# A decoder layer on one core: score products on 64 rows of the array, and a tile's turned queries copied in one operation

## What is computed

```python
q = (x @ Wq + bq).reshape(1, B * N, H, hd)          # H = 16 heads of hd = 16
kv = (cond @ Wkv + bkv).reshape(1, -1, 2, H, hd)
...
q = _fq_sym(q, axis=-1)      # per query and head: integers of -127..127 times a scale
k = _fq_sym(k, axis=-1)
v = _fq_sym(v, axis=2)
attn = jnp.einsum('bhqd,bhkd->bhqk', q, k)          # 2048 queries x 2048 keys, per head
attn = jax.nn.softmax(attn.astype(jnp.float32), axis=-1)
attn = _fq_unsigned(attn, axis=-1)
out = jnp.einsum('bhqk,bhkd->bhqd', attn, v)
```

## Time and profile before

| | |
|---|---|
| runs shown | 1208.26, 1210.47, 1211.15 us |
| median | 1210.47 us |
| the profiled execution's own time | 1209.02 us |
| its span on the core | 1207.2 us |
| VectorE, TensorE, ScalarE, GpSimd busy | 82%, 79%, 73%, 69% |
| TensorE's granted clock, mean | 0.955 of full speed |

### The profile page before, as it was taken

The page is one execution under the profiler, slowest core; times in us unless marked ns, Lnnn a source line. Parts: engine busy times, 40 slices in busy tenths (PEclk is TensorE's granted clock), DMA queues, the critical chain, the costliest instruction groups (busy, mean ns, idle before and its releaser), DMA issues.

```text
span 1207.2 us, 30185 instructions
## 1 busy us (share of the span) xinstructions
PE 958.1 (79%) x11255; PEld 700.0 (58%) x11424; DVE 989.7 (82%) x1865; ACT 884.3 (73%) x1085; POOL 838.9 (69%) x890
## 2 busy tenths in 40 slices
PE   7966678787887878787887878787887878778886
PEld 4644446565665656566665656565665656656565
DVE  4878778797988878797988878797988878798983
ACT  2636677778787778778787778777787777778782
POOL 7678777777777887777877887777777877733030
PEclk9967899899999999999999999899999989999997
DMA  5001000000000000000000000000000000000000
GB/s 200 2 35 40 6 1 6 2 10 2 6 7 5 7 1 11 2 6 6 6 6 7 6 2 10 1 6 6 6 7 6 7 1 6 2 6 2 6 2 10
DMA packets 8439, 14.00 MB, mean 12 GB/s; under 512 B 1635, under 2 KB 6246, under 8 KB 7910
## 3 DMA queue, kind: packets, MB, share of 16 engines
q1 hardware_dynamic: 8294, 12.06, 3.0%
HBM read 9.96 MB, written 2.10 MB: 10 GB/s over the span
## 4 chain that ended last, share of the span: by engine, by line
PE 40%; ACT 20%; issue 19%; DVE 17%; POOL 2%; DMA 0%; DVEq 0%; ACTq 0%; SPq 0%; POOLq 0%
PE ps_score L1479 10%; DVE score L1103 10%; PE ps_score L1468 9%; ACT prob L797 9%; ACT prob_t L809 8%; PE ps L1332 7%; PE ps_pv L1495 5%; DVE prob_t L1120 2%; PE ps_score L1332 2%; DVE early L1170 2%; ACT routed_both L848 1%; PE ps L1421 1%; ACT queries L782 1%; DVE stats L1026 1%; PE ps L1518 1%
## 5 line engine op out<-in xcount | busy, mean ns | idle before, releaser
L1103 DVE TENSOR_SCALAR_CACHE_REDUCE score<-ps_score,q_neg 128x1024 f32<-128x1024 f32 x512 | 642.9, 1278 | 147.9 <-PE ps_score L1468 145.4
L797 ACT ACTIVATE prob<-score,exp_bias 128x2048 uint16<-128x2048 f32 x256 | 513.9, 2007 | 14.9 <-DVE exp_bias L1113 14.9
L1468 PE MATMUL ps_score<-keys,queries 128*128 128x512 bf16 x855 | 281.5, 396 | 193.4 <-ACT prob_t L809 121.5
L1479 PE MATMUL ps_score<-ident_f,prob 128*128 128x128 f16 x4096 | 280.7, 223 | 16.7 <-ACT prob L797 8.8
L1479 PEld LDWEIGHTS ps_score<-ident_f,prob 128*128 128x128 f16 x4096 | 250.9, 100 | 50.2 <-ACT prob L797 22.5
L809 ACT COPY prob_t<-ps_score 128x1024 int32<-128x1024 int32 x192 | 194.3, 1012 | 55.2 <-PE ps_score L1479 53.3
L1468 PEld LDWEIGHTS ps_score<-keys,queries 128*128 128x128 bf16 x1024 | 68.3, 99 | 258.2 <-issue 162.7
L543 POOL TENSOR_TENSOR folded<-product 128x512 f32<-128x512 f32 x128 | 160.0, 1273 | 6.3 <-DVE ho L1062 4.3
L533 POOL TENSOR_TENSOR product<-hs_exp,v_tok 128x1024 f32<-128x1024 f32 x64 | 148.8, 2348 | 12.3 <-ACT hs_exp L765 12.3
L533 POOL TENSOR_TENSOR product<-qk_rot 128x1024 f32<-128x1024 f32 x64 | 148.9, 2347 | 4.0 <-POOL qk_rot L526 4.0
L1495 PEld LDWEIGHTS ps_pv<-prob_t,values 128*32 128x32 f16 x4096 | 114.8, 97 | 54.5 <-issue 54.4
(11 more groups left out here) (145 smaller groups left out, 1256.6 us busy)
## 6 DMA issues: line engine op xcount, KB each, us to landing
prob_t<-in_w SPq DMA_DIRECT2D x3, 1024.0 KB, 4.8
x_in<-in_x SPq DMA_DIRECT2D x16, 128.0 KB, 2.0
score<-in_cond_t SPq DMA_DIRECT2D x4, 512.0 KB, 6.8
out<-x_out SPq DMA_DIRECT2D x16, 128.0 KB, 1.7
w_qkv<-in_w_qkv SPq DMA_DIRECT2D x1, 768.0 KB, 4.0
early<-in_w_kv SPq DMA_DIRECT2D x1, 512.0 KB
w_s<-in_w_s SPq DMA_DIRECT2D x3, 128.0 KB
w_o<-in_w_o SPq DMA_DIRECT2D x1, 256.0 KB
```

The lines of the kernel that those rows point to most:

```text
L797: act.activation(prob[:, s, :].bitcast(U16), score[:, s, :], ACT.Exp, bias=exp_bias[:, s:s + 1], scale=-1.0, accum_out=prob_sum[:, t.par, ...
L1103: dve.tensor_scalar(score[:, s, HALF * i:HALF * i + HALF], ps_score[:, slot(h, i)].rearrange("p b k -> p (b k)"), q_neg[:, t.par, h:h + 1] ...
L1468: mm = pe.matmul(ps_score[:, slot(h, i), b, :], queries[:, t.par, h // 2, h % 2, :], keys[:, h // 2, k0:k0 + KEYS], start=True, stop=True)
L1479: mm = pe.transpose(out[:, P * i:P * i + P], prob[:, h % RING, P * i:P * i + P], ident_f16[:])
```

## The change

The score products read 48 partitions of keys and queries, 0 to 47 for an even head and 64 to 111 for an odd one; in the built program each of them uses 64 rows of the array by 128 columns, rows 0 to 63 or 64 to 127. `queries` loses its axis j and its zeros, the memset with its semaphore goes, and `keep_queries` is one copy of 128 partitions. `q_kept` counts one per tile where it counted two.

```diff
-        queries = sb("queries", [P, 2, H // 2, 2, P], BF16)
+        queries = sb("queries", [P, 2, H // 2, P], BF16)
...
-            pool.memset(queries[:].rearrange("p r a j q -> p (r a j q)").bitcast(F32), 0.0).then_inc(rows_cleared, 1)
...
-                if t.starts():
-                    act.wait_ge(rows_cleared, 1)
-                for j in range(2):
-                    rows = slice(P // 2 * j, P // 2 * j + P // 2)
-                    act.copy(queries[rows, t.par, :, j, :], bank_bf[5][rows, :].rearrange("p (a q) -> p a q", q=P)
-                             ).then_inc(q_kept, 1)
+                act.copy(queries[:, t.par].rearrange("p a q -> p (a q)"), bank_bf[5]).then_inc(q_kept, 1)
...
-                    pe.wait_ge(q_kept, t.count(2, 2))
+                    pe.wait_ge(q_kept, t.count(1, 1))
...
+                rows = slice(P // 2 * (h % 2), P // 2 * (h % 2) + 3 * HD)
                 for b in range(2):
                     k0 = HALF * i + KEYS * b
-                    mm = pe.matmul(ps_score[:, slot(h, i), b, :], queries[:, t.par, h // 2, h % 2, :],
-                                   keys[:, h // 2, k0:k0 + KEYS], start=True, stop=True)
+                    mm = pe.matmul(ps_score[:, slot(h, i), b, :], queries[rows, t.par, h // 2, :],
+                                   keys[rows, h // 2, k0:k0 + KEYS], start=True, stop=True)
```

More of the change, by code:

```diff
@@ L309, in layer_kernel @@
         q_kept = sem("q_kept")
-        rows_cleared = sem("rows_cleared")
         sum_inverted = sem("sum_inverted")
@@ L1553, in experts @@
                     if (t + 2).exists():
-                        pe.wait_ge(q_kept, (t + 2).count(2, 2))
+                        pe.wait_ge(q_kept, (t + 2).count(1, 1))
                 if i == 1 and j == 1:
```

## The result

The changed kernel takes 1262.0 us (median of four runs, 1257.7 to 1275.5) against 1210.6 us before: 1.045 times as long, with a 95% interval of 1.041 to 1.049. The forecast was slower, 1228 us, with a range up to 1252; the loss is 51.4 us where 17.5 were predicted.

What follows compares the result with a forecast made beforehand. No engine alone bounds the kernel; the chain of waits does, TensorE on 40% of it. 1209.0 - 15.8 + 29.1 + 4.5 = 1226.8, plus 1.5 to the median: 1228 us; own range 1214 to 1245, with rivals 1204 to 1252.

Steps and rivals of the forecast that it cites:

- the copy: ScalarE at h = 13: one of two turned-queries copies goes, 1.0 us a tile, wholly on the path, -15.8 us.
- Its cover on TensorE's side: q_turn and gate product, next to become late, are delayed 0.2 us; copies start from an exponential's end, without idle time.
- The memset's 1.8 us: GpSimd at 5.2 us of the span loses this work, but the loads hide it: 0.
- The price of a place: TensorE, each change of array shape: +0.11 us with 16-bit weights behind it, +0.19 us with float32 weights.
- How many places are on the path: Shape changes on the chain: 63 entries after 128 x 128 products, 125 exits (105 float32, 20 16-bit), +29.1 us.
- a tenth of the work off the chain: Of the other 46 us of shape changes, where the chain runs over VectorE and ScalarE, one tenth counts: +4.5 us.
- the clock: Rival: half-row products make TensorE's granted clock fall more often, about 1.1 us a tile, 18 us: 1246 us; chance 0.10.
- No price for 64 rows: Rival: 64-row score products on TensorE need no priced change of shape, so the kernel takes 1195 us; chance 0.11.
- the draw: Rival: float32 exits cost 0.11 and waits cover half the places; 10 us added, about 1210 us; chance 0.12.
- Weights in the open within a pair: Rival: second score product's weight load isn't hidden, 0.05 to 0.1 us per pair, +7 to +15, about 1239 us; chance 0.07.

Runs made afterwards that it cites:

- VectorE's half and the filling: Kernel before, with VectorE copying the upper 64 partitions of turned queries and 8 unread products added at h = 15 of each tile: 1182.8 us, 0.978.
- the split copy: Kernel before, with VectorE copying the upper 64 partitions of the turned queries at the end of h = 14, ScalarE the lower: 1200.2 us, 0.992.

## Why the prediction was right and wrong

**What bounds the kernel; the copy.** Right. One copy of 1.00 us instead of two, the whole block behind it moves forward, and the stall keeps its 3.33 us. The term was -15.8 us (16 x 1.0 is 16.0; the 0.2 matters nowhere). Undoing it costs some 14 in the changed kernel, and tiles at full clock go from 67.34 to 66.20 with the one copy and to 66.18 with VectorE's half and the filling, 1.16 a tile or 18.6 us for 16. Its cover on TensorE's side (q_turn and the gate product) held, with no idle time ahead of the copy at 645.65. The memset's 1.8 us went into a wait: GpSimd stands 8.3 us ahead of `rope`'s first step where it stood 6.6.

**The price of a place.** Right, to 0.01 us: 0.11 with 16-bit weights, predicted 0.19 and found 0.20 with float32. It was carried over from 32 rows and 32 columns, and 64 rows and 64 columns pay the same. The weight load of a score product no longer comes ahead of it, as was foretold: before, it began 0.05 us ahead (load at 617.68 us, product at 617.73), and now both begin at 672.92. The Trainium skill, "TensorEngine Tiling (Array Packing)", Key Properties, says that changing the tiling mode drains TensorE. The pieces of 0.54 us for 64 rows and 0.55 us for 64 columns agree with it.

**How many places are on the path.** Right in the sum, by a count that was off. Of the 63 entries counted on the chain of before, 13 follow the values products, where the shape changed already, so only 50 are new and the term is 1.4 us too large. Predicted 29.1 + 4.5 = 33.6 us; at equal clock the places cost 32.8 us, as columns, and for 64 rows a full-clock tile is 68.02 us against 66.18 without them, 1.84 a tile or 29.4 us. The judgement that a tenth of the work off the chain gets through, the weakest step of the sum, was near enough. That the full-clock tile stands for the whole is an extrapolation from the middle of the span. The profile after was to show full-clock tiles near 67.34 + 1.1 us; it is 67.34 + 0.68.

**The step that failed: the clock.** The sum puts it at nothing, on the ground that the stall keeps its length; as a rival it has a price of 18 us, where about 40 came out. As an estimate from tiles at full clock, the changed kernel would be at about 1210.6 + 16 x 0.68 = 1221 us. The other 40 or so are the clock's, which agrees with the 40 us between 64 rows with two copies (1275.7) and 64 columns with two copies (1235.7). The stall did keep its length, at 3.33 us, and the falls did not: behind it the clock stayed down for up to 10.2 us instead of up to 6.8, and with 64-row products it also fell where there is no stall, behind 3.40 us in which TensorE was busy for 2.74. So the premise was right and the step from it to the clock was wrong. The copy and the places, which the sum was made of, held; a forecast by the places alone could only come near the 1221 us. And I took the price from the middle tiles, while a part of the loss, 17 of the 49 us between the profiled executions, lies outside them: the first stretch, from 73.3 to 77.5 us, and the end, from the last queries copy on, 100.7 us before and 113.2 us after:

```profile
1106.54:1207.20 100.66, 77.74 (x967) 0.93 0.02 5
```

```profile
1142.79:1256.00 113.21, 94.53 (x980) 0.82 0.02 5
```

**The rivals.** No price for 64 rows, and the draw: fallen, by the pieces of 0.54 and 1.06 us. Weights in the open within a pair: fallen, two score products add 0.54 behind a turn, the same 0.11 over the streaming as before behind the values products. The clock: right in kind, and less than half of the price. Its way, that the clock falls more often, is part of what happened; that it stays down longer was not thought of. I never asked what the array did while the clock stood low, only how long TensorE had stood still before.

**What stays open.** With 65 rows on an unchanged shape the clock costs 9 us, with 48 rows and the changes of shape some 40. How much of the difference comes from 48 instead of 65 rows, and how much from the two acting together, no run separates. With 65 rows, too, TensorE had stood for 1.7 us or more of the 3.4 us ahead of every fall between 200 and 1100 us, so that the falls without a stall are seen with 64-row products alone. Nor is it shown why tiles of 68.26 us recur one after another, in the kernel before as in the one with the split copy.

## What to carry to other kernels

Small products on a part of the array stream no faster, and each change of the array's shape in an alternating order costs a tenth of a microsecond, two with float32 weights behind it. Two products on 64 columns each, side by side, took together the time of one on all (0.55 us for four, 0.54 for two on 64 rows); whether 64-row products side by side gain anything, no run here tests. Whoever takes rows, columns or time from TensorE should look at the granted clock stretch by stretch, since both a gain (the copy's, by half or more) and a loss can be changed by it as much as by the work itself. Where a stall lets the clock fall, a few products that nobody reads can be worth more than the work that they add: here 8 of them, with a copy moved into VectorE's own stall, gave 28 us.

## What the runs showed of the hardware

- The granted clock answers to how many rows a product takes, not only to how long TensorE is busy. With score products on 65 rows instead of 128, in the same order on the same shape, its mean fell from 0.955 to 0.936 in the profiled executions, for 9 us; rows that hold zeros did as much for it as others (tiles of 68.26 and 68.24 us at 0.95). With 64 columns beside 64 columns at every score product it was 0.968, with the same changes of shape at which 64 rows had 0.914.
- With 64-row score products the clock can stay at 1.2 GHz while TensorE is busy without a gap (3.40 of 3.40 us, twice in a row), and it can fall behind 3.40 us of which TensorE was busy for 2.74. In the kernel before, between 200 and 1100 us of the span, it rose behind every gapless stretch, and ahead of every fall TensorE had stood for 1.9 us or more of 3.4.
- A change of the array's shape costs the same for 64 rows and 64 columns as for 32: 0.11 us until the next 16-bit product streams, 0.20 with float32 weights.
- A copy of 1024 bf16 columns out of PSUM takes 1.00 us on ScalarE from 64 partitions and from 128.
- Gains through the clock are not additive: 9 us and 5 us alone, 28 us together.
